# Short convolutions of four taps: VectorE steps replaced by diagonal matmuls summed in PSUM, in the mamba and delta-rule layers of a 16-layer network

## The reference

```python
# mamba: 256 channels
xz = x @ in_proj_w;  xs, z = split(xz)
xs = silu(causal_depthwise_conv4(xs, conv_w) + conv_b)
# then: dt, B, C from xs @ x_proj_w; selective scan over the tokens with 16 states;
# y = scan + D * xs;  out = (y * silu(z)) @ out_proj_w

# delta rule: 3 x 128 channels
def _short_conv(x, w):                       # w: 128 x 4
    xp = jnp.pad(x, ((0, 0), (K - 1, 0), (0, 0)))
    y = sum((xp[:, j:j + x.shape[1], :] * w[:, j] for j in range(K)))
    return _silu(y)
q, k, v = (_short_conv(h @ W.T, w) for W, w in ...)
beta = max(sigmoid(h @ b_w.T), 1e-6)
# then: the chunked delta rule on q, k, v, beta; two more causal filters of v, of 5 and of 64 taps;
# a gating network mixes the four results
```

## Time and profile before

| | |
|---|---|
| median of 3 runs | 3241.55 us (3233.91 to 3244.31) |
| the profiled execution | 3234.41 us, span 3233.1 us, mean granted TensorE clock 0.882 |
| TensorE matmul busy | 2661.0 us, 82% |
| VectorE busy | 2186.1 us, 68% |
| ScalarE busy | 1378.1 us, 43% |
| GpSimd busy | 572.6 us, 18% |

### The profile page before, as it was taken

The page is one execution under the profiler, slowest core; times in us unless marked ns, Lnnn a source line. Parts: engine busy times, 40 slices in busy tenths (PEclk is TensorE's granted clock), DMA queues, the critical chain, the costliest instruction groups (busy, mean ns, idle before and its releaser), DMA issues.

```text
span 3233.1 us, 41018 instructions
## 1 busy us (share of the span) xinstructions
PE 2661.0 (82%) x15734; PEld 1723.3 (53%) x15734; DVE 2186.1 (68%) x4115; ACT 1378.1 (43%) x2436; POOL 572.6 (18%) x482
## 2 busy tenths in 40 slices
PE   5789897886788678989788878869878989778888
PEld 1256674453485323766454448659845455444554
DVE  6987888998999899988699876651174243552331
ACT  5533336563552453333365555441134335334342
POOL 2700001115690054000011108200010100000000
PEclk8999997787887689989788779869989999789899
DMA  3000001110000000000211110007400000000000
GB/s 146 0 1 1 1 1 34 33 37 8 1 1 1 0 1 0 1 33 1 69 34 33 27 59 1 1 1 227 132 1 2 0 2 1 7 1 1 1 2 7
DMA packets 51924, 73.18 MB, mean 23 GB/s; under 512 B 5776, under 2 KB 41360, under 8 KB 51088
## 3 DMA queue, kind: packets, MB, share of 16 engines
q1 hardware_dynamic: 51728, 70.56, 7.2%
HBM read 52.32 MB, written 1.44 MB: 17 GB/s over the span
## 4 chain that ended last, share of the span: by engine, by line
PE 39%; DVE 16%; issue 5%; ACT 3%; POOL 1%; DMA 0%; SPq 0%; DVEq 0%; POOLq 0%; ACTq 0%
PE ps L108 35%; PE ps L111 3%; DVE wide_q L138 3%; DVE conv L135 2%; DVE state L141 2%; DVE inverse L147 1%; DVE qk L129 1%; POOL long L129 1%; DVE stream_a L132 1%; DVE outT L144 1%; DVE stats L153 1%; DVE x L129 1%; DVE turned L129 0%; DMA turned<-conv 0%; ACT L120 0%
## 5 line engine op out<-in xcount | busy, mean ns | idle before, releaser
L108 PEld LDWEIGHTS ps<-held_ffn,hidden 128*128 128x128 f32 x2304 | 298.4, 191 | 160.1 <-issue 108.6
L121 ACT ACTIVATE grown<-ps,bias_grown 128x512 f32<-128x512 f32 x288 | 198.0, 688 | 324.9 <-PE ps L108 318.1
L108 PE MATMUL ps<-held_ffn,hidden 128*128 128x128 f32 x2304 | 306.6, 276 | 22.1 <-DVE hidden L135 22.1
L129 POOL TENSOR_TENSOR qk<-conv,held_const 128x512 f32<-128x512 f32 x64 | 93.0, 1455 | 1030.2 <-DVE conv L135 1030.2
L135 DVE SCALAR_TENSOR_TENSOR conv<-conv_in,held_l1a,conv 128x512 f32<-128x512 f32 x288 | 207.5, 738 | 29.4 <-ACT conv L121 26.0
L129 POOL TENSOR_TENSOR long<-long,product 128x512 f32<-128x512 f32 x136 | 199.3, 1502 | 155.5 <-ACT product L121 154.9
L135 DVE SCALAR_TENSOR_TENSOR hidden<-ps,bias_kept,grown 128x512 f32<-128x512 f32 x288 | 210.7, 745 | 3.3
L132 DVE TENSOR_SCALAR grown<-grown,bias_fallen 128x512 f32<-128x512 f32 x288 | 139.2, 484 | 83.7 <-ACT grown L121 82.8
L138 DVE TENSOR_REDUCE wide_q<-ps 128x4 f32<-128x512 f32 (+1 forms) x128 | 114.4, 954 | 95.6 <-PE ps L108 95.6
L129 POOL TENSOR_TENSOR part<-state,c_rows 128x512 f32<-128x512 f32 x128 | 162.4, 1297 | 85.8 <-issue 48.5
L159 POOL MEMSET wide_q<- 128x1536 f32 x8 | 11.0, 1378 | 925.5 <-ACT rstd L121 925.5
(11 more groups left out here) (440 smaller groups left out, 5820.2 us busy)
## 6 DMA issues: line engine op xcount, KB each, us to landing
ring<-lags SPq DMA_DIRECT2D x64, 512.0 KB, 4.5
turned<-conv SPq DMA_DIRECT2D x256, 64.0 KB, 2.0
held_ffn<-in_ffn SPq DMA_DIRECT2D x1, 4690.0 KB, 18.7
held_l1a<-in_l1a SPq DMA_DIRECT2D x2, 2120.0 KB, 15.7
held_l3f<-in_l3f SPq DMA_DIRECT2D x1, 2824.0 KB, 12.2
held_rows<-in_rows SPq DMA_DIRECT2D x1, 1044.5 KB, 8.0
out<-x SPq DMA_DIRECT2D x4, 256.0 KB, 2.6
held_const<-in_const SPq DMA_DIRECT2D x1, 785.0 KB, 4.9
```

The source lines that it names most:

```text
L108: return self.sent(self.real.matmul(out, lhsT, rhs, **kw), cost, 0.15)
L121: return self.sent(self.real.activation(out, a, func, **kw), cost)
L129: return self.vector(self.real.tensor_tensor(out, a, b, op), columns(out))
```

## The change

In mamba and in the delta rule the four steps on VectorE are replaced. ScalarE makes for each chunk and tap a 128x128 matrix with the channel's tap on its diagonal (identity times a per-partition scale; `tap_made`). TensorE multiplies it with the shifted `conv_in` and sums the four taps in one PSUM bank, the one in which the projection lay before it was copied. ScalarE's Silu reads this bank; in mamba it adds the bias `conv_b` as well. Mamba has a buffer for all 8 diagonals. The delta rule has 12 diagonals and 8 places in what is later `square`; the last four wait until a place is free (`tapped`). In mamba the diagonals stand ahead of the first copy on ScalarE, in the delta rule after the third. In mamba the small projections `x_proj`, which write the same two banks, now wait until both chunks are active, where they waited for one at a time.

```diff
 def mamba(m, st, x):
...
-                    bc_mid=([96, TOK], BF16), thrice=[P, ED, 3 * 2 * N])
+                    bc_mid=([96, TOK], BF16), thrice=[P, ED, 3 * 2 * N], taps=[P, 4 * ED, P])
...
+        yield pe.wait_ge(s.cleared, 1)
+        for c in range(ED):
+            yield pe.wait_ge(s.copied, c + 1)
+            for j in range(4):
+                yield pe.wait_ge(s.tap_made, 4 * c + j + 1)
+                mm = pe.matmul(st.ps(c), c_.taps[:, 4 * c + j, :], c_.conv_in[:, c, :, j:j + T], start=(j == 0),
+                               stop=(j == 3))
+            mm.then_inc(s.convolved)
         yield pe.wait_ge(s.thrice, ED)
-        yield pe.wait_ge(s.copied, ED)
+        yield pe.wait_ge(s.active, ED)
         for c in range(ED):
-            yield pe.wait_ge(s.active, c + 1)
...
         yield act.wait_ge(m.load["l0a"], 16)
+        yield act.wait_ge(m.load["const"], 16)
+        for j in range(4 * ED):
+            act.activation(c_.taps[:, j, :], m.ident, ACT.Copy, scale=w.conv_w[:, j:j + 1]).then_inc(s.tap_made)
...
         for c in range(ED):
-            yield act.wait_ge(s.convolved, 4 * (c + 1))
-            act.activation(b.xs[:, c, :], conv[:, c, :], ACT.Silu).then_inc(s.active)
+            yield act.wait_ge(s.convolved, c + 1)
+            act.activation(b.xs[:, c, :], st.ps(c), ACT.Silu, bias=w.conv_b[:, c:c + 1]).then_inc(s.active)
...
-        yield ve.wait_ge(s.cleared, 1)
-        step = Steps(s.convolved)
-        for c in range(ED):
-            yield ve.wait_ge(s.copied, c + 1)
-            out = seqs(conv[:, c, :])
-            yield step(ve.tensor_scalar(out, c_.conv_in[:, c, :, 0:T], w.conv_w[:, 4 * c:4 * c + 1],
-                                        w.conv_b[:, c:c + 1], ALU.mult, ALU.add))
-            for j in range(1, 4):
-                yield step(ve.scalar_tensor_tensor(out, c_.conv_in[:, c, :, j:j + T],
-                                                   w.conv_w[:, 4 * c + j:4 * c + j + 1], out, ALU.mult, ALU.add))
...
 def delta_rule(m, st, x):
...
+    TAPS = 8
...
+    taps = c.square[:, :, :, :].rearrange("p r t n -> p (r t) n")
...
+        yield pe.wait_ge(s.cleared, 2)
+        for r in range(3):
+            yield pe.wait_ge(s.copied, r + 1)
+            for i in range(4):
+                yield pe.wait_ge(s.tap_made, 4 * r + i + 1)
+                mm = pe.matmul(st.ps(r), taps[:, (4 * r + i) % TAPS, :], c.conv_in[:, r, :, i:i + T], start=(i == 0),
+                               stop=(i == 3))
+                mm.then_inc(s.tapped)
...
         yield act.wait_ge(s.cleared, 2)
+        yield act.wait_ge(m.load["l1b"], 16)
+
+        def tap(k):
+            if k >= TAPS:
+                yield act.wait_ge(s.tapped, k - TAPS + 1)
+            act.activation(taps[:, k % TAPS, :], m.ident, ACT.Copy, scale=w.d_taps[:, k:k + 1]).then_inc(s.tap_made)
+
+        for k in range(TAPS):
+            yield from tap(k)
         for r in range(3):
-            yield act.wait_ge(s.convolved, 4 * (r + 1))
+            for k in range(4 * r + TAPS, min(4 * r + 4 + TAPS, 12)):
+                yield from tap(k)
+            yield act.wait_ge(s.tapped, 4 * (r + 1))
             if r < 2:
-                act.activation(c.conv[:, r, :], c.conv[:, r, :], ACT.Silu).then_inc(s.active)
+                act.activation(c.conv[:, r, :], st.ps(r), ACT.Silu).then_inc(s.active)
             else:
-                act.activation(b.v_in[:, :, PAD:], seqs(c.conv[:, r, :]), ACT.Silu).then_inc(s.v_active)
+                act.activation(b.v_in[:, :, PAD:], seqs(st.ps(r)), ACT.Silu).then_inc(s.v_active)
...
-        yield ve.wait_ge(s.cleared, 2)
-        step = Steps(s.convolved)
-        for r in range(3):
-            yield ve.wait_ge(s.copied, r + 1)
-            out = seqs(c.conv[:, r, :])
-            yield step(ve.tensor_scalar(out, c.conv_in[:, r, :, 0:T], w.d_taps[:, 4 * r:4 * r + 1], None, ALU.mult))
-            for i in range(1, 4):
-                yield step(ve.scalar_tensor_tensor(out, c.conv_in[:, r, :, i:i + T],
-                                                   w.d_taps[:, 4 * r + i:4 * r + i + 1], out, ALU.mult, ALU.add))
```

More of the change, by code:

```diff
@@ L398, in mamba @@
     ED, N, RANK = 2, 16, 64
-    L = Layer(m, NORM + "projected copied gated cleared convolved active low_made low_copied stepped pick thrice bc "
+    L = Layer(m, NORM + "projected copied gated cleared tap_made convolved active low_made low_copied stepped pick thrice bc "
               "absolute decayed logged rectified delta rate dx b_spread c_spread c_copied blank decay drive state part "
@@ L408, in mamba @@
     c_ = first.many(conv_in=[P, ED, SEQS, 3 + T], soft=[P, ED, TOK], low=[RANK, TOK], bc_rest=[96, TOK],
-                    bc_mid=([96, TOK], BF16), thrice=[P, ED, 3 * 2 * N])
+                    bc_mid=([96, TOK], BF16), thrice=[P, ED, 3 * 2 * N], taps=[P, 4 * ED, P])
     d = then.many(c_rows=[P, 2, TOK], decay=[P, ED, 2, TOK], state=[P, 2, ED, TOK],
                   part=[P, 3, TOK])
-    xT, conv, y = st.xT, b.xs, b.dx
+    xT, y = st.xT, b.dx
     drive = lambda c: st.ps(1 - c)
@@ L1235, in delta_rule @@
     G = NT * H
-    L = Layer(m, NORM + "projected copied cleared convolved active v_active beta_made beta_open beta shorts longs scaled "
+    L = Layer(m, NORM + "projected copied cleared tap_made tapped active v_active beta_made beta_open beta shorts longs scaled "
               "filtered turned_qk turned_v taken taken_v squared sums shifted_n root normed kb turned_again taken_again "
@@ L1311, in tensor @@
         yield pe.wait_ge(s.longs, BY_VECTOR - BY_PE + 1)
-        L.past(pe, "projected beta_made turned turned_v filtered turned_again turned_f")
+        L.past(pe, "projected tapped beta_made turned turned_v filtered turned_again turned_f")
         for t in range(NT):
@@ L1429, in scalar @@
         act.activation(o.src[:, 0, :, :], st.tiles(0), ACT.Copy).then_inc(s.taken_f)
-        L.past(act, "copied active v_active beta_open taken taken_v squared scaled taken_again taken_f")
+        L.past(act, "copied tap_made active v_active beta_open taken taken_v squared scaled taken_again taken_f")
         for t in range(NT):
@@ L1502, in vector @@
         yield ve.wait_ge(s.turned_again, 3)
-        L.past(ve, "cleared convolved beta sums shorts normed kb longs")
+        L.past(ve, "cleared beta sums shorts normed kb longs")
         for t in range(NT):
```

## The result

The changed kernel takes 3298.68 us (median of 4 runs, 3298.42 to 3308.64) against 3242.93 for the kernel before, measured beside it (3233.91 to 3245.40): a ratio of 1.0192, 95% interval 1.0174 to 1.0210. It is 56 us slower. The forecast was 3225 us, with a range that ended at 3256.

The account below looks back on a forecast made before the run. VectorE was taken as the limit in the first delta stage, TensorE as near it in the second. Terms -17 - 7 + 8 - 1 = -17 us, from the median 3241.55, gave 3225 us, range 3192 to 3256.

Parts of the forecast that it names:

- Prices: All four stages: a tap costs TensorE 0.87 us, a diagonal ScalarE 0.32; VectorE loses 54.8 us, TensorE gains 69.7.
- Mamba 1, +8: First mamba stage: taps and second stream's projections queue on TensorE, loop starts near 60 us; +8 (0 to +12).
- Mamba 2, -7: Second mamba stage: taps fill idle TensorE, chunk active near 1118 us, loop starts 6 to 8 us earlier; -7.
- Refilled: Rival, 22 in 100: VectorE's freed time goes to the filters' background preparation and to waits; about 3241 us.
- Delta 1, -17: First delta stage: GpSimd handover 11 us earlier, plus 6 us from streams reaching GpSimd apart; 17 gained (4 to 30).
- The bill: First delta stage: TensorE's work from 787 us sums to 60.5 us, so handover at 850 instead of 861.4.
- The stagger: First delta stage: first stream reaches GpSimd 15 to 20 us ahead, background work fills VectorE's gap; worth 6 us.
- Delta 2, -1: Second delta stage: same TensorE work costs +5 us, against first stream starting GpSimd 12 us earlier; -1 (-8 to +8).
- The rival of TensorE's queue: Rival, 18 in 100: second stream's matmuls wait behind first's taps, 10.4 us a delta stage, 7 a mamba; 3259 us.
- Low clock: Rival, 5 in 100: taps follow idle time, half of the 80 cost 0.87 us more, +35; 3259 us.
- Full relief: Rival, 13 in 100: VectorE bounds all of the first half, 49 us come off; 3193 us.

Follow-up runs that it names:

- experiments 10 to 12: VectorE part of the filters' preparation held until both first delta stages end: kernel before 3275.16 us, changed kernel 3305.98, changed kernel with stream a held at both delta stages 3310.22.
- delta 2 alone: Kernel before with diagonals in the second delta stage only (pairs 2 and 3): 3253.91 us.
- experiment 4: The run with delta 2 alone, diagonals in the second delta stage only against the kernel before: 3253.91 us.
- In step: Diagonals in the second delta stages only, plus a TensorE wait so each stream's recurrence starts when the other is ready too: 3266.51 us.
- a held once: Changed kernel plus a VectorE wait: stream a's second delta stage starts only when stream b has finished the channel mix before it; 3274.48 us.

## Why the prediction was wrong

- **Prices (right for one operation, off in the sum).** 0.88 us a tap against 0.87; eight diagonals in 2.43 us, 0.30 each against 0.32. But VectorE was relieved by 40.1 us of busy time where 55 were announced, and TensorE loaded by 73.8 where 60 to 70 were.
- **Mamba 1, +8 (right).** +7.6 / +9.9; the loop's first step at 62.38, "about 60".
- **Mamba 2, -7 (right in size by luck).** The changed kernel has -3.3 / -8.4. With its diagonals alone, the chunk is active at 1117.67 as forecast (near 1118), but the loop starts 4.2 us later against the stage's entry (1145.00 from 1094.5; 1142.11 from 1095.8) and the stage takes 6.5 / 6.7 us more. In the changed kernel the loop starts 5.7 us earlier, but with diagonals in delta 1 alone 7.3 us earlier, with VectorE's steps: b comes further behind in both, and its absence is the likely help. What holds the loop in the first case I didn't test; in its trace VectorE works 16.8 us on the filters' preparation between the chunk's activation and the loop's start (6.1 us before), which is what *Refilled* described.
- **Delta 1, -17 (failed).** The step was "the handover to the long filter's tail on GpSimd comes at 861.4 us: 11 us gained". GpSimd's first step came at 869.7 us and its last at 986.9, where before 845 and before 960 were the signs. Against the entry, the handover moved by -2.3 us for a and +9.8 for b. The bill added up TensorE's matmuls as if they were what the handover waits for. The chain behind v (transposes, square, norm, scaling) stayed and VectorE's own filter steps ran until it, to 868.16 and 882.40. The stagger came (14.2 us) and brought nothing: `wT` is copied at +0.4 / +4.4 and the rest comes behind it. "Refilled", my reading for this, didn't survive experiments 10 to 12; the wait behind the norm was read, not tested.
- **Delta 2, -1 (failed; the term that decides).** Its parts came close: in the run with delta 2 alone, stream b's v is active at 1912.6 (near 1915) and the last GpSimd step at 2037.4 (near 2040). In the changed kernel they came at 1945.8 and 2068.8, since b enters 28.0 us later. What failed is the step that ended the sum at the GpSimd tail: I costed everything behind it, and the distance that the stages before hand on, at nothing, since no edit touches the one and the sum had no term for the other. Measured in the changed kernel: +45.9 / +41.4 us.
- **What delta 2 had in its place.** Shown is the distance: without any diagonal a larger one costs 31 / 22 us beyond its hold, delta 1's diagonals alone bring 39.0 / 11.2 us to this stage by it, and holding a takes 24 us off the changed kernel. Shown beside it, with the `wT` copies 5 to 7 us apart: the order that the planner writes for the recurrence is worth 9 to 13 us a stage at nearly equal clock, in both directions, and in one run the same order at the half clock cost some 22 us more. Not explained are the 14.4 / 16.8 us ahead of the `wT` copies; in the three other runs with diagonals in delta 2 alone this part is 4.8 to 6.9 us longer than before for a and 5.3 to 9.5 for b, where the run of experiment 4 has -2.9 / +0.7. That any new order moves a stage by several microseconds is a rival for such small terms, and it isn't excluded.
- **The rival of TensorE's queue** named the right place: b's v comes 12.5 us later against its entry in delta 2 alone (36.9 us, 24.4 before), but only 1.4 later in delta 1, so its own test, 10 us in both, isn't met. Its 3259, which lay outside the range that ended at 3256, took the delay as it stood; the later stages made more of it. *Low clock* looked for it in the taps, in whose stretches the clock was 0.99 (26 to 62 us) and 0.87 (784 to 868); in the run with delta 2 alone it fell to 0.50 some 150 us behind the first taps. *Full relief* was argued from VectorE at 95 to 99% in three stretches; the earlier trace rows has two such, the third is at 88%.

Still open: why the recurrence keeps the half clock in one run and not in another of the same order of groups (64.4 against 42.0 us); what the waits that force the step cost elsewhere; what makes the part of delta 2 ahead of `wT` longer; and why b loses 9 us in the channel mix behind delta 1. Holding a explains 24 of the changed kernel's 56 us; the rest is attributed stage by stage from the trace and was not taken away by any run.

## What to carry to other kernels

Where two streams share in-order queues, the order in which their small dependent steps interleave is worth as much as the steps: after any change ahead of it, compare the groups of such a loop (here x8 against x4, x2, x2) before trusting a sum of busy times. A delay given to the second stream is not paid once: streams that stand apart lose what each hid for the other. Price what the distance and the order become, and the clock in them. And follow the stage to its exit in the sum, through the parts that the diff doesn't touch.

## What the runs showed of the hardware

- TensorE can show as busy for 10.00 of 10 us over 40 us and stay at a granted 0.50 (delta 2 alone, 2055 to 2095 us). In step it rose to 0.99, with 16 identity matmuls more per stream it stood at 0.94 over the recurrence, and in the split order itself it stood at 0.92 with a held once. The Trainium skill ("TensorE: Matmul & The Clock Gate", section "A second HAM failure mode: psum-queue depth-cycling") tells of frequent short idle times between groups of matmuls with which the clock goes back and forth between half and full. These traces don't settle whether that is at work here: the same groups ran at 0.55 in one run and at 0.92 in another, and the idle times don't show, as busy time is modelled at 10.00.
- An identity matmul of 128 columns put into the chain of the recurrence cost 0.66 us each in delta 1 (0.83) and 0.41 in delta 2 (0.94), where four transposes in a row take 0.60 us, 0.15 each.
- A kernel's executions can spread by 22 us (3236.83 to 3259.20) with nothing changed.
